# Cross-attention and a routed feed-forward layer: one division cut in two, one batch's projection in halves, and a wait for each half of the scores

## The chip, the cores and the metric

The kernel runs on one core of a Trainium2 chip. The metric is the device time of one execution in microseconds (us), of which the median of three runs is taken. A core has five engines with their own instruction streams: TensorE (PE; PEld is its weight load), VectorE (DVE), ScalarE (ACT), GpSimd (POOL) and SyncE (SP, which only issues transfers here). They wait for each other through semaphores.

## What is computed

Eight batches of 512 tokens of width 256 attend with 16 heads of width 16 to 1024 context tokens. Then the 128 best of the 512 tokens of each batch pass through a small transformer layer (causal attention among themselves, gated feed-forward of width 682) and replace their rows.

```python
x = x + xattn(layernorm(x), ctx, mask)          # 8 batches, 512 queries, 1024 keys, 16 heads of 16
#   q, k, v = x @ wq.T, ctx @ wk.T, ctx @ wv.T;  softmax(q k^T / 4) v;  @ wo.T
y = layernorm(x)
idx = top_k(y @ w_router, 128);  s = y[idx]
s = s + attention(rmsnorm(s, g1)) @ W_out.T     # causal, 128 tokens
s = s + (silu(h @ W1.T) * (h @ W2.T)) @ W3.T    # h = rmsnorm(s, g2)
out = x + y.at[idx].set(s)                       # y with the 128 chosen rows replaced
```

## The kernel before

**A batch is 32 steps.** A step `s` belongs to one group of four heads (`g = s // 8`) and one tile of 128 keys (`t = s % 8`). On PE it is, in this order: the scores of step `s` (`pe_scores`, L464: four heads, each in two column tiles, 32 rows by 64 columns of the array, into two of three pairs of PSUM banks); the values of step `s - 1` (`pe_values`, L486: four matmuls over all 128 rows, accumulated in `o_bank` over the eight key tiles); and then the "slot": work of the next batch's projections ("P"), of the same batch's late ones ("I", in batch 0 alone), or of the previous batch's feed-forward ("F"), which the table `PE_SLOT` (`PE_SLOT_0` for batch 0) puts at a step's number. ACT does the two exponentials of a step (`act_scores`, L506, one per pair of banks, 128x1024 each), and then what `ACT_SLOT` names. DVE follows `DVE_ORDER`, POOL `POOL_ORDER`. All orders are written out by hand, and every engine works strictly in its order.

**The ring of banks.** The three pairs are used in turn, two a step (`ring`, L443). The first pair of step `s` was last read by the second exponential of step `s - 2`, the second pair by the first exponential of step `s - 1`. Before L479 PE waits for both pairs; the values of step `s - 1` wait for the second exponential of step `s - 1` (L491).

**The slot's bank.** All work in slots goes through one bank, `m_bank` (`MISC`, 7). `take_bank` (L279) waits until the copy of the work before has freed it: ACT for keys ("K00" to "K11") and transposes ("xT", "hidT"), DVE for values ("V0" to "V3"), queries ("Q0", "Q1") and most of the feed-forward.

**The projection of the next batch** is ten products of 16 or 32 matmul records (4 K, 4 V, 2 Q) and two sets of transposes (xT). From batch 1 on, five of them are split over two steps (":0" and ":1"); in batch 0 each stands whole in one step, and of the steps 8 to 30 ten have a product, two have transposes, and 11 have nothing.

**The division.** `dve_norm` (L580) is done once for each group, after its last values: DVE transposes `o_bank` into `o_blk` and frees `o_bank`, takes the reciprocal of the sums, multiplies, and for an odd group transposes the result into `o_t`, which only the product with `wo` in the next batch reads. The division of group 1 ("norm1") falls into step 16. In the same step PE makes the feed-forward's keys ("k"), and in step 17 its values ("v"), its scores ("fs"), and the next batch's "V2". DVE's order is q, norm1, k, so that the copy of "k" out of `m_bank` (L773) comes after all four operations of norm1, and "v" needs that bank.

**The context** of a batch is loaded into one buffer, `ctx_in`, as soon as the last product that reads it has been copied out ("K10" and "V3" each add one to `ctx_free`), and read again by "K00:0" in step 31.

## Time and profile before

| what | value |
|---|---|
| median of three runs | 895.89 us (893.83 to 895.96) |
| the profiled execution | 896.05 us, its span 894.3 us |
| PE busy | 852.3 us, 95% of the span |
| ACT busy | 569.8 us, 64% |
| DVE busy | 313.4 us, 35% |
| POOL busy | 123.5 us, 14% |
| granted TensorE clock, mean | 0.993 of 2.4 GHz |

How to read it: PE is busy nearly everywhere up to the last batch's end, and the question for each microsecond is whether PE had an instruction that it could start. The step is the unit: the start of one step's scores to the next one's. The last 66 us, in which the last batch's feed-forward runs alone, are no part of the change.

### The profile page before, as it was taken

How to read it: one execution, taken by the hardware profiler on the slowest of the kernel's cores; microseconds unless marked ns; L12 is line 12 of the kernel's file. 1: busy time of each engine (PE TensorE's matmuls, PEld its weight loads, DVE VectorE, ACT ScalarE, POOL GpSimd, SP SyncE). 2: the span in 40 equal slices, each digit the busy share in tenths (PEclk: the TensorE clock that was granted, in tenths of full speed). 3: DMA queues.
4: the chain of work that ended last, by engine and by line, in shares of the span. 5: the costliest groups of instructions: out<-in, count | busy, mean ns of one | idle time of the engine just before them, and what ended most of it. 6: DMA issues, size and time to landing. Idle time of an engine off the chain costs nothing. (4 is left out here: it accounts for less than half of the span.)

```text
span 894.3 us, 28250 instructions
## 1 busy us (share of the span) xinstructions
PE 852.3 (95%) x11779; PEld 294.9 (33%) x11785; DVE 313.4 (35%) x918; ACT 569.8 (64%) x644; POOL 123.5 (14%) x175
## 2 busy tenths in 40 slices
PE   7999999999999999999999999999999999989774
PEld 2322232324323332334323333234323342224343
DVE  3132135421552226421553316422354214411631
ACT  3566767676677767666577766676576766776110
POOL 4000102020120102120120101101121100210110
PEclk9999999999999999999999999999999999999898
DMA  5060201210011200111011200102001100200000
GB/s 183 17 227 1 78 3 31 55 58 24 7 37 49 79 8 27 59 32 49 9 37 49 79 8 25 45 20 78 7 10 53 31 8 2 61 1 4 7 25 9
DMA packets 27577, 35.56 MB, mean 40 GB/s; under 512 B 2083, under 2 KB 24142, under 8 KB 27448
## 3 DMA queue, kind: packets, MB, share of 16 engines
q1 hardware_dynamic: 24952, 31.73, 11.2%
q0 software_dynamic: 2496, 1.98, 1.4%
q8 instruction: 96, 1.57, 0.7%
q14 instruction: 33, 0.27, 0.1%
HBM read 27.53 MB, written 8.93 MB: 41 GB/s over the span
## 5 line engine op out<-in xcount | busy, mean ns | idle before, releaser
L511 ACT ACTIVATE probs<-pair_bank 128x1024 f32<-128x1024 f32 x512 | 496.3, 1021 | 225.4 <-ACTq L510 225.4
L481 PE MATMUL pair_bank<-q_sb,k_sb 32*64 32x512 f32 x4096 | 286.4, 612 | 10.0 <-PEq L478 9.6
L500 PE MATMUL o_bank<-probs,va 128*32 128x512 f32 x2048 | 273.3, 604 | 1.3 <-ACT probs L511 1.1
L500 PEld LDWEIGHTS o_bank<-probs,va 128*32 128x32 f32 x2048 | 41.5, 108 | 205.4 <-issue 114.2
L481 PEld LDWEIGHTS pair_bank<-q_sb,k_sb 32*64 32x64 f32 x4096 | 60.9, 129 | 145.0 <-issue 145.0
L266 PE MATMUL m_bank<-wv_sb,ctx_in 128*32 128x256 f32 x1024 | 61.5, 380 | 0.0
L266 PE MATMUL m_bank<-ctx_in,wk_sb 128*32 128x512 f32 x480 | 60.3, 592 | 0.0
L628 DVE TENSOR_SCALAR va<-m_bank,valid 128x256 f32<-128x256 f32 x64 | 28.1, 480 | 91.6 <-DVEq L625 91.6
L586 DVE STREAM_TRANSPOSE o_blk<-o_bank 128x512 f32<-128x512 f32 x32 | 22.9, 717 | 92.7 <-DVEq L585 92.7
L266 PEld LDWEIGHTS m_bank<-hid_t,w 128*32 128x32 f32 x1392 | 39.5, 110 | 17.0 <-issue 16.0
L266 PEld LDWEIGHTS m_bank<-wv_sb,ctx_in 128*32 128x32 f32 x1024 | 33.5, 110 | 34.2 <-issue 18.9
L266 PE MATMUL m_bank<-hid_t,w 128*32 128x128 f32 x1392 | 43.3, 273 | 0.5 <-PEq L281 0.5
L896 POOL DMA_INDIRECT in_order<-y_tok,place x28 | 29.2, 1044 | 68.3 <-POOLq L895 58.2
L904 POOL DMA_INDIRECT out_dram<-att,row_of x8 | 13.2, 1647 | 171.3 <-POOLq L903 171.3
L888 POOL TENSOR_SCALAR_AFFINE_SELECT p_f<-p_f 128x1024 f32<-128x1024 f32 x16 | 17.5, 1094 | 123.8 <-POOLq L886 122.8
L266 PE MATMUL m_bank<-xn_t,wq_sb 128*32 128x512 f32 x240 | 30.7, 592 | 0.0
L872 POOL TENSOR_TENSOR mask_in<-mask_in,mask_row 128x256 int32<-128x256 int32 x32 | 23.4, 765 | 46.3 <-POOLq L869 46.3
L276 PE MATMUL o_bank<-before 128*128 128x512 bf16 x95 | 26.4, 435 | 3.3 <-POOL before L988 2.7
L798 DVE STREAM_TRANSPOSE o_blk<-m_bank 128x512 f32<-128x512 f32 x8 | 5.7, 717 | 65.1 <-DVEq L797 65.1
L266 PE MATMUL m_bank<-wo,o_t 128*32 128x256 f32 x448 | 27.1, 380 | 0.4 <-PEq L281 0.4
L266 PEld LDWEIGHTS m_bank<-ctx_in,wk_sb 128*32 128x32 f32 x480 | 15.3, 110 | 36.2 <-issue 36.2
L826 DVE SCALAR_TENSOR_TENSOR silu<-half_tanh,m_bank 128x384 f32<-128x384 f32 x15 | 8.3, 554 | 47.7 <-DVEq L825 47.7
(173 smaller groups left out, 604.1 us busy)
## 6 DMA issues: line engine op xcount, KB each, us to landing
ctx_in<-in_ctxT SPq DMA_DIRECT2D x7, 1024.0 KB, 5.0
x_in<-in_x SPq DMA_DIRECT2D x8, 512.0 KB, 4.0
x<-in_x SPq DMA_DIRECT2D x8, 512.0 KB, 4.3
mask_in<-in_mask SPq DMA_DIRECT2D x8, 512.0 KB, 3.9
out_dram<-base SPq DMA_DIRECT2D x8, 512.0 KB, 5.5
ctx_in<-in_ctxT SPq DMA_DIRECT2D x2, 512.0 KB, 7.5
mask_row<-in_mask SPq DMA_DIRECT2D x8, 128.0 KB, 3.9
x_tok<-in_order SPq DMA_DIRECT2D x7, 128.5 KB, 2.0
```

What stands on the lines that cost most here:

```text
L266: last = nc.tensor.matmul(dst[j], a[:, j], c, start=(begins and n == 0), stop=(ends and n == len(pairs) - 1))
L276: last = nc.tensor.matmul(dst, before[:, 0, 0:P], before[:, 1], start=True, stop=True)
L481: last = nc.tensor.matmul(pair_bank[pairs[r // 2]][j:j + 64, r % 2], key_tile(b, s, r)[:, j:j + 64], query_tile(b, s, r), start=True, stop ...
L500: last = nc.tensor.matmul(o_bank[32 * r:32 * r + 32], va[b % 2][:, t, HV * h:HV * h + 32], probs[s % 2][:, r], start=(t == 0), stop=(t == ...
L511: nc.scalar.activation(probs[s % 2][:, 2 * e:2 * e + 2, :], pair_bank[p][:], ACT.Exp, scale=HD ** -0.5).then_inc(s_free[p], 1)
L586: nc.vector.transpose(o_blk[:], o_bank[:]).then_inc(o_free, 1)
L628: last = nc.vector.tensor_scalar(by_head(va[b % 2][:, t])[:, :, 0:HD], bank[i][:, e * D:(e + 1) * D].rearrange("p (h d) -> p h d", h=H), o ...
L826: nc.vector.scalar_tensor_tensor(out=silu2[r][:], in0=half_tanh[r][:], scalar=1.0, in1=bank[i][:, 0:3 * P], op0=ALU.add, op1=ALU.mult).the ...
L872: last = nc.gpsimd.tensor_tensor(mask_words[:, t * WORDS:(t + 1) * WORDS], mask_words[:, t * WORDS:(t + 1) * WORDS], first, ALU.subtract)
L888: last = nc.gpsimd.affine_select(out=half, in_=half, compare_op=ALU.is_ge, fill=0.0, base=0, pattern=[[0, H8], [1, CAP]], channel_multipli ...
L896: nc.gpsimd.indirect_dma_start(in_order[:], bass.IndirectOffsetOnAxis(place[t][:, 0:1], 0), y_tok[:, t], None, bounds_check=CAP - 1, oob_i ...
L904: nc.gpsimd.indirect_dma_start(out.rearrange("b s d -> (b s) d"), bass.IndirectOffsetOnAxis(row_of[:, 0:1], 0), att[:], None, compute_op=A ...
```

## The change

It has three parts. First, "norm1" in `DVE_ORDER` becomes "norm1a" (the transpose out of `o_bank`), then "k", then "norm1b" (the other three operations). Second, `PE_SLOT_0` puts the projection of batch 1 in halves over the steps 8 to 29, one half a step, with a new `part` for V (the bank is taken by the first half, the signal given by the second); the transposes stand alone in steps 18 and 21; ACT's and DVE's tables follow. Third, in `pe_scores` the wait for the second pair of banks moves behind the first half's matmuls.

```diff
-             ("F", "base"), ("F", "q"), ("N", "norm1"), ("F", "k"), ("P", "V2"), ...
+             ("F", "base"), ("F", "q"), ("N", "norm1a"), ("F", "k"), ("N", "norm1b"), ("P", "V2"), ...

-             ..., ("I", "Q1", 6, False), ("P", "K00", 8, False), ("P", "K01", 9, False),
-             ("P", "K10", 10, False), ("P", "K11", 11, False), ("P", "V0", 12, False), ("P", "V1", 13, False),
-             ("P", "xT0", 15, False), ("P", "xT1", 17, False), ("P", "V2", 18, False), ("P", "Q0", 19, False),
-             ("P", "V3", 21, False), ("P", "Q1", 23, False), ("X", "K00:0", 31, False)]
-ACT_SLOT_0 = [("I", "K10", 2), ("I", "K11", 4), ("P", "K00", 8), ("P", "K01", 9), ("P", "K10", 10), ("P", "K11", 11),
-              ("P", "xT0", 15), ("P", "xT1", 17), ("P", "differ", 20)]
+             ..., ("I", "Q1", 6, False), ("P", "K00:0", 8, False),
+             ("P", "K00:1", 9, False), ("P", "K01:0", 10, False), ("P", "K01:1", 11, False), ("P", "K10:0", 12, False),
+             ("P", "K10:1", 13, False), ("P", "K11:0", 14, False), ("P", "K11:1", 15, False), ("P", "V0:0", 16, False),
+             ("P", "V0:1", 17, False), ("P", "xT0", 18, False), ("P", "V1:0", 19, False), ("P", "V1:1", 20, False),
+             ("P", "xT1", 21, False), ("P", "V2:0", 22, False), ("P", "V2:1", 23, False), ("P", "Q0:0", 24, False),
+             ("P", "Q0:1", 25, False), ("P", "V3:0", 26, False), ("P", "V3:1", 27, False), ("P", "Q1:0", 28, False),
+             ("P", "Q1:1", 29, False), ("X", "K00:0", 31, False)]
+ACT_SLOT_0 = [("I", "K10", 2), ("I", "K11", 4), ("P", "K00", 9), ("P", "K01", 11), ("P", "K10", 13), ("P", "K11", 15),
+              ("P", "xT0", 18), ("P", "differ", 20), ("P", "xT1", 21)]
-DVE_ORDER_0 = [..., ("P", "stats"), ("N", "norm0"), ("P", "xn"), ("P", "V0"),
-               ("P", "V1"), ("N", "norm1"), ("P", "V2"), ("P", "Q0"), ("P", "V3"), ("P", "Q1"), ("N", "norm2")]
+DVE_ORDER_0 = [..., ("P", "stats"), ("N", "norm0"), ("P", "xn"),
+               ("N", "norm1"), ("P", "V0"), ("P", "V1"), ("P", "V2"), ("N", "norm2"), ("P", "Q0"), ("P", "V3"), ("P", "Q1")]

             elif stage[0] == "V":
-                dst = take_bank(pe, i)
-                for e in range(2):
+                dst = bank[i] if part == 1 else take_bank(pe, i)
+                for e in share(part, 2):
...
-                last.then_inc(done["V"], 1)
+                if part != 0:
+                    last.then_inc(done["V"], 1)

             pairs = [ring(b, s, e) for e in range(2)]
-            for p in pairs:
-                pe.wait_ge(s_free[p], 1)
-                pe.sem_inc(s_free[p], -1)
             for r in range(HG):
+                if r % 2 == 0:
+                    pe.wait_ge(s_free[pairs[r // 2]], 1)
+                    pe.sem_inc(s_free[pairs[r // 2]], -1)
                 for j in range(0, P, 64):

-        def dve_norm(dve, b, g):
+        def dve_norm(dve, b, g, part=""):
-            dve.wait_ge(o_ready, 1)
-            dve.sem_inc(o_ready, -1)
-            nc.vector.transpose(o_blk[:], o_bank[:]).then_inc(o_free, 1)
-            dve.drain()
+            if part != "b":
+                dve.wait_ge(o_ready, 1)
+                dve.sem_inc(o_ready, -1)
+                nc.vector.transpose(o_blk[:], o_bank[:]).then_inc(o_free, 1)
+                dve.drain()
+            if part == "a":
+                return
```

## Rows read from the trace of the kernel before

**Rows 1.** Busy time by stretch: batch 0's steps 8-30, batch 1, batch 7.

```profile
46.92:116.29 69.37, 66.11 (x784) 17.47 (x785) 14.67 (x41) 48.99 (x55) 4.09 (x6) 1.00 0.25 86
119.19:222.38 103.19, 102.45 (x1460) 35.33 (x1456) 38.28 (x112) 70.71 (x81) 14.87 (x19) 1.00 0.12 37
735.36:828.00 92.64, 85.87 (x1224) 27.75 (x1224) 27.77 (x80) 66.37 (x73) 10.67 (x14) 1.00 0.07 18
```

**Rows 2.** PE's waits, whole span: us in total, times, longest us.

```profile
PE pair_bank L481 <- PEq L478: 9.6, 29, 1.3
PE m_bank L266 <- PEq L281: 3.6, 7, 0.7
```

**Rows 3.** Timeline, batch 0: scores of steps 20 (bare), 21 (whole V3), 22.

```profile
87.10 1.11 PE L481 MATMUL pair_bank<-q_sb,k_sb 32*64 32x512 f32 x16
...
89.51 1.12 PE L481 MATMUL pair_bank<-q_sb,k_sb 32*64 32x512 f32 x16 [0.30 <-PEq L478]
...
93.28 1.11 PE L481 MATMUL pair_bank<-q_sb,k_sb 32*64 32x512 f32 x16
```

**Rows 4.** Timeline, batch 1, PE alone: a step with half a product (Q1:0).

```profile
157.02 1.11 PE L481 MATMUL pair_bank<-q_sb,k_sb 32*64 32x512 f32 x16
158.07 1.07 PE L500 MATMUL o_bank<-probs,va 128*32 128x512 f32 x8
158.95 1.04 PE L266 MATMUL m_bank<-xn_t,wq_sb 128*32 128x512 f32 x8
159.92 1.11 PE L481 MATMUL pair_bank<-q_sb,k_sb 32*64 32x512 f32 x16
```

**Rows 5.** Timeline, batch 0: one bare step of a run of seven.

```profile
104.27 1.12 PE L481 MATMUL pair_bank<-q_sb,k_sb 32*64 32x512 f32 x16 [0.29 <-PEq L478]
105.32 1.06 PE L500 MATMUL o_bank<-probs,va 128*32 128x512 f32 x8
105.51 1.94 ACT L511 ACTIVATE probs<-pair_bank 128x1024 f32<-128x1024 f32 x2 [0.46 <-ACTq L510]
106.68 1.12 PE L481 MATMUL pair_bank<-q_sb,k_sb 32*64 32x512 f32 x16 [0.29 <-PEq L478]
```

**Rows 6.** Timeline, batch 7, step 17: scores that stood still in the middle.

```profile
780.86 1.07 PE L481 MATMUL pair_bank<-q_sb,k_sb 32*64 32x512 f32 x4
...
782.36 1.10 PE L481 MATMUL pair_bank<-q_sb,k_sb 32*64 32x512 f32 x12 [0.43 <-issue]
...
783.40 1.06 PE L500 MATMUL o_bank<-probs,va 128*32 128x512 f32 x8
```

**Rows 7.** Timeline, steps 16 and 17 of batch 1, then of batch 3.

```profile
170.44 0.72 DVE L586 STREAM_TRANSPOSE o_blk<-o_bank 128x512 f32<-128x512 f32 x1 [1.16 <-DVEq L585]
...
172.11 1.07 PE L500 MATMUL o_bank<-probs,va 128*32 128x512 f32 x8
...
173.34 0.42 DVE L773 COPY k_f<-m_bank 128x256 f32<-128x256 f32 x1 [0.55 <-DVEq L772]
...
173.92 1.07 PE L266 MATMUL m_bank<-wqkv,hid_t 128*32 128x256 f32 x16 [0.74 <-PEq L281]
...
377.71 1.07 PE L500 MATMUL o_bank<-probs,va 128*32 128x512 f32 x8
...
379.16 1.07 PE L266 MATMUL m_bank<-wqkv,hid_t 128*32 128x256 f32 x16 [0.39 <-PEq L281]
```

**Rows 8.** Timeline, batch 7: norm0, the chosen rows' norm, their transposes.

```profile
760.49 0.72 DVE L586 STREAM_TRANSPOSE o_blk<-o_bank 128x512 f32<-128x512 f32 x1 [1.27 <-DVEq L585]
...
773.57 0.48 DVE L757 SCALAR_TENSOR_TENSOR hid<-x_tok,ms,g_b 128x256 f32<-128x256 f32 x1 [1.24 <-DVEq L756]
...
774.66 0.44 PE L257 MATMUL m_bank<-ident,hid 128*128 128x128 f32 x2
```

**Rows 9.** Timeline, batch 0, step 20: ACT's check of the mask.

```profile
90.17 1.06 ACT L533 ACTIVATE mask_in<-mask_in 128x1024 f32<-128x1024 int32 x1
```

**Rows 10.** Page, transfers: the context's load, KB and us to landing.

```profile
ctx_in<-in_ctxT SPq DMA_DIRECT2D x7, 1024.0 KB, 5.0
```

More of the change, by code:

```diff
@@ L65 @@
              ("F", "order1"), ("N", "norm0"), ("F", "order2"), ("F", "order3"), ("P", "Q0"), ("P", "V1"), ("F", "selected"), ("P", "Q1"),
[1 row of a table removed]
[1 row of a table added]
              ("N", "norm2"), ("F", "u0"), ("F", "w0"), ("F", "u1"), ("F", "w1"), ("F", "down")]
 PE_SLOT_0 = [("I", "V0", 0, False), ("I", "V1", 1, False), ("I", "K10", 2, False),
[4 rows of a table removed]
-ACT_SLOT_0 = [("I", "K10", 2), ("I", "K11", 4), ("P", "K00", 8), ("P", "K01", 9), ("P", "K10", 10), ("P", "K11", 11),
-              ("P", "xT0", 15), ("P", "xT1", 17), ("P", "differ", 20)]
-DVE_ORDER_0 = [("I", "V0"), ("I", "V1"), ("I", "V2"), ("I", "V3"), ("I", "Q1"), ("P", "stats"), ("N", "norm0"), ("P", "xn"), ("P", "V0"),
-               ("P", "V1"), ("N", "norm1"), ("P", "V2"), ("P", "Q0"), ("P", "V3"), ("P", "Q1"), ("N", "norm2")]
[7 rows of a table added]
+ACT_SLOT_0 = [("I", "K10", 2), ("I", "K11", 4), ("P", "K00", 9), ("P", "K01", 11), ("P", "K10", 13), ("P", "K11", 15),
+              ("P", "xT0", 18), ("P", "differ", 20), ("P", "xT1", 21)]
+DVE_ORDER_0 = [("I", "V0"), ("I", "V1"), ("I", "V2"), ("I", "V3"), ("I", "Q1"), ("P", "stats"), ("N", "norm0"), ("P", "xn"),
+               ("N", "norm1"), ("P", "V0"), ("P", "V1"), ("P", "V2"), ("N", "norm2"), ("P", "Q0"), ("P", "V3"), ("P", "Q1")]
 POOL_ORDER = [("F", "var"), ("P", "var"), ("F", "scatter"), ("F", "rms0"), ("F", "causal"), ("F", "rms1"), ("P", "differ"), ("F", "add")]
@@ L1094, in _ @@
                         elif kind == "N":
-                            dve_norm(dve, b, int(stage[4]))
+                            dve_norm(dve, b, int(stage[4]), stage[5:])
                         elif kind in ("P", "I"):
```

4 rows, old and new, of tables (DVE_ORDER, PE_SLOT_0) are left out of this document.

## The prediction, made before the changed kernel was run

> **What bounds the kernel now.** I read the busy times by stretch first. Batch 1 is a wall of PE work: 102.45 us of 103.19 [rows 1]. The steps 8 to 30 of batch 0 leave 69.37 - 66.11 = 3.3 us, and batch 7, which has no next batch to project for, leaves 92.64 - 85.87 = 6.8 us [rows 1]. So there is something to win in batch 0, in batch 7, and in whatever small wait each batch between still has. PE's own waits name them: 9.6 us in 29 waits for a pair of banks (L478), and 3.6 us in seven waits for `m_bank`, most of them one in each batch's step 17 [rows 2]. Then the timeline, with the start of each step's scores as the ruler. In batch 0 a step with nothing in its slot takes 89.51 - 87.10 = 2.41 us, one with a whole product 93.28 - 89.51 = 3.77 us [rows 3], and in batch 1 one with half a product 159.92 - 157.02 = 2.90 us [rows 4]. Two halves take 5.80 us, a whole and a bare step 6.18 us: a bare step is not PE's pace.
>
> Why it is not: scores start at 104.27, ACT's first exponential at 105.51 (1.24 us later), and the next step's scores at 106.68, which is 1.17 us after that exponential started and so just when it had freed the pair of banks [rows 5]. 1.24 + 1.17 = 2.41 us is a loop between PE and ACT. PE's own part is 1.05 us from scores to values [rows 5] and 0.88 us from values to what follows [rows 4], 1.93 us.
>
> **Part 1, batch 0 in halves.** All ten products become two halves in two steps, no matmul is added. Before, the stretch of steps 8 to 30 takes 69.37 us [rows 1]. After, it holds 20 steps with a half at 2.90 us [rows 4] and three others. The transposes stand alone in a step before and after, so their price cancels; so does the one step that stays bare (30). What is left is ten times (one whole plus one bare against two halves): 10 x (6.18 - 5.80) = 3.8 us, and by the rounded starts 3.7 us. Against it stands one collision. ACT's check of the mask (1.06 us, with its accumulator read some 1.3 us) [rows 9] now stands in step 20 beside half a product, and the short step 21 (transposes only) follows. ACT then has 1.94 + 1.3 us of work and 0.2 us of start against a 2.90 us step, so it falls some 0.5 us behind, and the scores of step 22 need its first exponential; the transposes' step leaves 0.2 to 0.3 us of this uncovered. Part 1: -3.7 + 0.3 = **-3.4 us**, between -3.8 and -2.5.
>
> What could be late there, one by one. The bank: a second half's copy by ACT starts after the second exponential and takes less than the scores and values (1.93 us) in front of the next half; batches 1 to 6 run the same pattern at 2.90 us [rows 4]. DVE: norm1 and norm2 now stand before V0 and Q0, each in the step in which its group ends, one step before the copy is due. The context: V3 moves from step 21 to 27, so the load for batch 2 is issued in step 28. It takes 5.0 us [rows 10]; K00:0 of step 31 comes three steps and 1.93 us after step 28's start, over 10 us, against some 1.3 + 5.0 us. Cover of 3 to 4 us; without it each microsecond late would be a microsecond. SP has nothing behind that load that batch 0 needs.
>
> **Part 2, norm1 around the copy of "k".** In batch 1 DVE transposes `o_bank` at 170.44 (0.72 us), then works off the other three operations, and copies "k" only at 173.34; "v" starts at 173.92, after PE stood still for 0.74 us [rows 7]. With the copy second, it can start when "k" is finished and the transpose is over, near 171.3, and ends near 171.8. The values of step 16 start at 172.11 and "v" could follow 0.88 us [rows 4] later, at 172.99: the wait is gone with 1 us to spare, and "v" moves 0.93 us. In batch 3 the same distance is 379.16 - 377.71 = 1.45 us instead of 0.88: 0.57 us [rows 7]. Batches 1 and 4 are of the first kind, 3, 5 and 6 of the second (2 too, though its values ran slow for another reason; I take 0.3). Batch 7 has no such wait: PE stood still for 1.5 us in the middle of its scores, with nothing to wait for (780.86 to 782.36) [rows 6], and the copy was done by then. What is late next: after "v" and "fs" V2 needs ACT's copy of "v", which now stands right behind the second exponential of step 17; I find it 0.1 to 0.2 us early. norm1b delays nobody: `o_t` is read a batch later, `o_bank` was freed by norm1a. Behind it on DVE waits V2's copy, 3 us later. Sum 2 x 0.93 + 3 x 0.57 + 0.3 = **-3.9 us**, between -2.5 and -4.5.
>
> **Part 3, a wait for each half.** It only matters where scores wait, that is in bare steps. The first half's pair was read by the second exponential of two steps before and is always free. The second half still starts at the old time, and the values behind it too: rows 6 show what values do when the second half of the scores comes late (782.36): they start at 783.40, 1.04 us later, no sooner, though the first half had run long before. So an isolated bare step wins nothing. The gain comes one step on: the first half of step s+1 is done early, so its first exponential starts right behind the second one of step s. Over two bare steps: exponential start, +1.17 second half, +1.04 values, +0.88 first half of the next, +1.24 its exponential = 4.33 us instead of 4.82. **0.48 us for each pair of neighbouring bare steps.** Batch 0 has after part 1 only single ones (7 and 30): nothing. Batches 1 to 6 have none. Batch 7: steps 18 and 19 are a pair (0.5 us); 21 and 23 are single; step 0 is followed by the product with `wo`, which waits for norm3 anyway. Steps 3 to 5 and 7 to 13 would give 1.9 us in four pairs, but behind them, in step 14, the transposes of the chosen rows wait for DVE and POOL: that chain runs from norm0 (760.49) to hid (773.57 + 0.48) and the transposes start at 774.66, 0.61 us after hid's end [rows 8]. The chain is set by norm0, that is by the values of step 7, which come 0.5 us earlier; of the 0.61 us a signal needs only some 0.15 (the second pair's wait above: 1.17 us less the exponential's 1.03), so another 0.45 us can go. Gain there 0.9 us, not 1.9. Part 3: **-1.4 us**, between 0 and -2.9.
>
> What the moved wait costs where nothing is waited for: no instruction is added, two of four stand four matmuls later. No row shows a wait in that place. PE idled before the scores in 29 of the 256 steps [rows 2]; in the other 227 two waits in a row cost nothing, so I take 0; bounds below.
>
> Sum: -3.4 - 3.9 - 1.4 = -8.7 us. The profiled execution took 896.05 us (span 894.3), so 887.35; it lies 0.16 above the median 895.89, so **887.2 us**. PE's clock is at its 2.4 GHz level in all three stretches (1.00) [rows 1] and is less idle after the change; I expect none of it to change.
>
> **Rivals.** (a) *The wait in the middle shows* (the slow side). Every step has its second wait between the matmuls of two heads. If PE's queue does not run ahead enough to hide it, each step pays. The price per step of which it decides: 8.7 / 256 = 0.034 us. The rows bound it between 0 (the 227 steps) and 0.29 us, the idle time of a bare step's wait [rows 5]; at 0.05 us it is +12.8 us, giving 900 us. Against: PE has 0.88 us of values and a slot in hand before each scores. The Trainium skill, "Advanced Engine Details and Errata" (Miscellaneous Facts, Network/Comms) gives 50 to 100 ns for a sequencer's read of a semaphore; if that stood in the open in each step, the estimate from that page would be 900 to 913 us. No row of this trace shows such a price in the open; if the 227 steps paid it, they hid it. (b) *The half waits give nothing*: values keep their time and batch 7 hangs on its chain of chosen rows throughout; 887.2 + 1.4 = 888.6. (c) *Batch 0 does not do what it says*: a copy out of `m_bank` or the context comes late and takes back most of part 1, 887.2 + 2.5 to 3.4 = 890.2. (d) *Batch 7's standstill of 1.5 us* [rows 6] was an accident of issue and falls elsewhere: 885.7. For it: nothing was waited for. Against: PE's instruction count before it is unchanged.
>
> **Chances.** Forecast 0.52, (a) 0.07, (b) 0.12, (c) 0.12, (d) 0.12, and 0.05 for less than a third of the gain, within 0.3% (2.7 us, about what a measurement of this kernel can tell from no change). The far ends of the three parts together give 896.05 - 11.2 - 0.16 = 884.7, and (d) could come on top, so the range begins at 884.2; it ends at (c) with part 2 at its small end as to one us, 891.2. That leaves out (a), the remainder and some of the tails. Faster by over 0.3% (below 893.2) 0.87, same 0.06, slower 0.07.
>
> **What would show it.** Right: batch 0's steps 8 to 30 span 66.0 us; `m_bank` waits at "v" gone (L281 from 3.6 us to near 0), step 17 at 5.87 us in batches 1 to 6; in batch 7's runs scores start in turns of some 1.9 and 2.4 us; PE idle at L257 before the transposes of step 14 in batch 7. Wrong: half steps longer than 2.90 us anywhere (rival a), a wait at L291 or L281 in batch 0 (rival c), batch 7 as long as before but for 0.5 us (b).

## The result, and the profile of the changed kernel

The changed kernel takes **887.21 us**, median of 4 runs (884.06 to 889.00); the kernel before, run beside it, 895.92 us (893.83 to 898.64). The ratio is 0.990, its 95% interval 0.9878 to 0.9922. The forecast was 887.2 us. The profiled execution of the changed kernel took 886.53 us, with a span of 884.8 us against 894.3 before.

Busy times by stretch, the same three stretches as in [rows 1], in the same columns (batch 0 from the scores of step 8 to those of step 31, batch 1, batch 7):

```profile
45.98:112.79 66.81, 66.72 (x788) 17.52 (x784) 15.05 (x42) 48.87 (x55) 4.08 (x6) 1.00 0.27 92
116.05:218.06 102.01, 102.01 (x1461) 35.25 (x1457) 38.30 (x112) 70.39 (x80) 14.85 (x19) 1.00 0.12 37
727.44:819.30 91.86, 89.40 (x1228) 29.72 (x1224) 27.78 (x80) 66.93 (x74) 11.04 (x14) 1.00 0.07 18
```

Batch 0's stretch went from 69.37 to 66.81 us and batch 1 from 103.19 to 102.01, with PE busy in all of it. Batch 7 went from 92.64 to 91.86. "Busy" needs care from here on: a group of matmuls counts as busy from its first start to its last end, so a stop in the middle of a group counts as work. Two such stops are told of below.

PE's waits, as in [rows 2] (us in total, times, longest us). The lines moved by 3 or 4: L485 is the scores' matmul (L481 before), L269 the products' (L266), L284 their wait (L281), L504 the values' (L500).

```profile
PE o_bank L504 <- issue: 1.3, 1, 1.3
PE m_bank L269 <- PEq L284: 1.1, 2, 0.6
PE pair_bank L485 <- PEq L483: 0.3, 1, 0.3
```

The 29 waits for a pair of banks (9.6 us) have become one of 0.3 us, and the seven for `m_bank` (3.6 us) two of 1.1 us in all. At the top stands a new one: 1.3 us ahead of the values, released by nothing ("issue").

Batch 1, steps 16 and 17, timeline of all engines (start, duration, engine, line, operation; idle time before it and what ended it in brackets), against [rows 7]:

```profile
167.07 0.72 DVE L591 STREAM_TRANSPOSE o_blk<-o_bank 128x512 f32<-128x512 f32 x1 [1.16 <-DVEq L590]
...
168.04 0.43 DVE L780 COPY k_f<-m_bank 128x256 f32<-128x256 f32 x1 [0.25 <-DVEq L779]
...
168.74 1.07 PE L504 MATMUL o_bank<-probs,va 128*32 128x512 f32 x8
...
169.62 1.05 PE L269 MATMUL m_bank<-wqkv,hid_t 128*32 128x256 f32 x16
```

The copy of "k" starts 0.97 us after the transpose instead of 2.90 us, and "v" (L269) follows the values by 0.88 us with no wait. Before it was 1.81 us, 0.74 of them a wait.

Batch 7, steps 3 to 5, a bare pair (3 and 4) with the wait at each half, against the bare step in [rows 5]:

```profile
738.36 1.11 PE L485 MATMUL pair_bank<-q_sb,k_sb 32*64 32x512 f32 x16
...
739.60 3.98 ACT L515 ACTIVATE probs<-pair_bank 128x1024 f32<-128x1024 f32 x4 [1.83 <-ACTq L514]
...
740.40 1.46 PE L485 MATMUL pair_bank<-q_sb,k_sb 32*64 32x512 f32 x16
...
742.78 1.11 PE L485 MATMUL pair_bank<-q_sb,k_sb 32*64 32x512 f32 x16
```

ACT runs four exponentials without a gap (3.98 us): the first half of the next scores was there in time. The scores start 2.04 and 2.38 us apart instead of 2.41 twice. The stretched 1.46 us of the second scores is the wait between its halves.

And the two stops. In batch 0, step 12, the scores take 2.26 us instead of 1.11, and the weight load in their middle stood 0.97 us with no wait that the profile names ("issue"). In batch 7, step 14, the values stop half way for 1.26 us, again with no named wait, and the transposes of the chosen rows (L260) come after them although `hid` (L764) had been ready since 766.08:

```profile
57.93 2.26 PE L485 MATMUL pair_bank<-q_sb,k_sb 32*64 32x512 f32 x16
...
59.12 0.19 PEld L485 LDWEIGHTS pair_bank<-q_sb,k_sb 32*64 32x64 f32 x3 [0.97 <-issue]
...
764.51 1.05 PE L504 MATMUL o_bank<-probs,va 128*32 128x512 f32 x4
...
765.60 0.48 DVE L764 SCALAR_TENSOR_TENSOR hid<-x_tok,ms,g_b 128x256 f32<-128x256 f32 x1 [1.24 <-DVEq L763]
...
766.82 1.05 PE L504 MATMUL o_bank<-probs,va 128*32 128x512 f32 x4 [1.26 <-issue]
...
767.80 0.44 PE L260 MATMUL m_bank<-ident,hid 128*128 128x128 f32 x2
```

The stop that the kernel before had in step 17 of batch 7 [rows 6] is gone.

Where the 9.5 us of span went, stretch by stretch. Each number is a difference between starts of scores in the two timelines; the experiments are shown for what follows (us; "b0 8-31" runs from the start of step 8 to that of step 31, and so on):

```
                  ahead  b0 0-8  b0 8-31  b0 31   b1      b2      b3      b4      b5      b6    b7 0-15 b7 15-20 b7 20-31 tail
before            18.74  28.18   69.37    2.90  103.19  102.63  102.62  102.97  102.62  102.14  39.67   17.51    33.14    68.58
changed           18.14  27.84   66.81    3.25  102.01  102.22  102.01  102.01  102.01  101.15  40.73   15.63    33.19    67.77
batch 0 alone     19.00  28.18   67.16    2.90  102.98  102.62  102.62  102.96  102.61  102.14  39.66   17.24    33.13    67.42
norm1 alone       18.34  28.18   69.37    2.90  102.24  102.47  102.03  102.03  102.02  101.54  39.66   16.69    33.60    68.19
half waits alone  18.05  27.84   68.08    3.24  103.12  102.60  102.60  102.95  102.60  101.74  39.15   16.22    33.31    68.50
no half waits     17.92  28.18   67.71    2.90  102.03  102.50  102.02  102.03  102.02  101.54  39.67   17.24    33.61    68.17
```

- *Batch 0 in halves:* -2.56 us, that is -3.70 us of its own and +1.14 us for the stop in step 12, which took 4.04 us where its neighbours take 2.90.
- *norm1 in two parts:* step 17 fell from 6.79 to 5.84 us in batches 1 and 4, from 6.44 to 5.84 in 3, 5 and 6, and by 0.4 to 6.06 in 2 (a short stop, 0.45 us before and 0.20 now, stands in that step): -4.1 us.
- *Step 1 of batch 1:* 4.12 to 3.91 us, -0.2 us. It goes with batch 0's new tables, not with norm1: e1 and e4 have 3.91, e2 still 4.12 (though e7, with all three parts, has 4.06).
- *Half waits:* the last step of batch 6 -0.37, batch 7's steps 0 to 14 -0.52 (39.67 to 39.15, read from the kernel with the half waits alone, which has no stop there), steps 15 to 19 -0.44 (17.51 less the old stop of 1.44 is 16.07, now 15.63): -1.33 us.
- *Stops:* one of 1.44 us went, two of 1.14 and about 1.5 us came: +1.2 us.
- *Outside the change:* -0.60 us ahead of the first scores and -0.81 us behind the last. In the tail the kernel before was granted a lower clock in that execution, 0.57 of full speed over 8 us against 1.00 in the same place of the changed kernel (PEclk is the third number from the end), so most of that stretch ran at the 1.2 GHz level (the other tails of the table, from 67.42 to 68.50, vary as much):

```profile
840.00:848.00 8.00, 6.42 (x20) 3.00 (x21) 7.28 (x31) 0.00 (x0) 0.00 (x0) 0.57 0.00 0
```
```profile
831.00:839.00 8.00, 6.02 (x29) 2.83 (x29) 7.47 (x31) 0.00 (x0) 0.00 (x0) 1.00 0.00 0
```

The first is before, the second the changed kernel. Sum: -3.7 - 4.1 - 0.2 - 1.3 + 1.2 - 1.4 = -9.5 us.

### The profile page after: what moved, and what is told of

Its sections match the earlier page's. It is cut to its first block and busy times, and to the rows that moved or that the text cites. A ratio compares the mean times of both kernels' runs of the same rounds, so it can differ in the third digit from the quotient of the medians.

```text
span 884.8 us, 28257 instructions
## 1 busy us (share of the span) xinstructions
PE 853.4 (96%) x11779; PEld 296.7 (34%) x11785; DVE 313.2 (35%) x918; ACT 569.6 (64%) x644; POOL 123.3 (14%) x175
## 5 line engine op out<-in xcount | busy, mean ns | idle before, releaser
L485 PE MATMUL pair_bank<-q_sb,k_sb 32*64 32x512 f32 x4096 | 291.3, 612 | 0.4 <-PEq L483 0.3
L504 PE MATMUL o_bank<-probs,va 128*32 128x512 f32 x2048 | 274.2, 604 | 2.7 <-issue 1.3
L504 PEld LDWEIGHTS o_bank<-probs,va 128*32 128x32 f32 x2048 | 41.7, 108 | 207.5 <-issue 112.9
L485 PEld LDWEIGHTS pair_bank<-q_sb,k_sb 32*64 32x64 f32 x4096 | 62.8, 129 | 134.6 <-issue 133.4
L269 PE MATMUL m_bank<-wv_sb,ctx_in 128*32 128x256 f32 x1024 | 62.2, 380 | 0.0
L269 PE MATMUL m_bank<-ctx_in,wk_sb 128*32 128x512 f32 x480 | 61.0, 592 | 0.0
L269 PEld LDWEIGHTS m_bank<-wv_sb,ctx_in 128*32 128x32 f32 x1024 | 33.4, 110 | 36.0 <-issue 21.3
L269 PEld LDWEIGHTS m_bank<-hid_t,w 128*32 128x32 f32 x1392 | 39.4, 110 | 17.2 <-issue 16.3
L269 PE MATMUL m_bank<-hid_t,w 128*32 128x128 f32 x1392 | 43.4, 273 | 0.5 <-PEq L284 0.5
L269 PE MATMUL m_bank<-xn_t,wq_sb 128*32 128x512 f32 x240 | 31.1, 592 | 0.0
L269 PE MATMUL m_bank<-wo,o_t 128*32 128x256 f32 x448 | 26.9, 380 | 0.6 <-PEq L284 0.6
L269 PEld LDWEIGHTS m_bank<-ctx_in,wk_sb 128*32 128x32 f32 x480 | 15.3, 110 | 36.2 <-issue 36.2
```

What stands on the lines that cost most here:

```text
L269: last = nc.tensor.matmul(dst[j], a[:, j], c, start=(begins and n == 0), stop=(ends and n == len(pairs) - 1))
L485: last = nc.tensor.matmul(pair_bank[pairs[r // 2]][j:j + 64, r % 2], key_tile(b, s, r)[:, j:j + 64], query_tile(b, s, r), start=True, stop ...
L504: last = nc.tensor.matmul(o_bank[32 * r:32 * r + 32], va[b % 2][:, t, HV * h:HV * h + 32], probs[s % 2][:, r], start=(t == 0), stop=(t == ...
```

## The experiments

Three sets, each on one chip with its own runs of the kernel before: 895.45 us in the first set (23 runs), 905.95 in the second (21, one of them an outlier of 2880.69 us), 904.28 in the third (7). The second and third sets ran on chips on which both kernels take some 9 us longer, so only ratios cross from one set to another. All kernels compute the whole result.

### First set: the three parts

**e1, batch 0 alone.** The new tables of batch 0 and "V" in halves; `norm1` whole, both waits ahead:

```
-   ("N", "norm1a"), ("F", "k"), ("N", "norm1b"),
+   ("N", "norm1"), ("F", "k"),
...
+            for p in pairs:
+                pe.wait_ge(s_free[p], 1)
+                pe.sem_inc(s_free[p], -1)
```

> Only batch 0's projection in halves, the rest as before. Theory A (fill): a half in a bare step costs 0.49 us over the bare 2.41, so ten pairs of whole and bare (6.18 us) become 5.80; steps 8 to 30 of batch 0 take 66.0 us instead of 69.4, or about 1.2 us more if PE stands still once without a wait as it did in the changed kernel (step 12: 4.04 instead of 2.90). Everything from batch 1 on is unchanged. Time 3.4 us below before, 2.2 with a standstill. Rival B: the gain of batch 0 in the changed kernel came from the half waits (steps 7 and 30 show 2.04 us there): then the stretch here would be above 68 us and the time within 1 us of before.

Measured: 893.03 us, ratio 0.9981 (0.9969 to 0.9993). Its stretch of steps 8 to 30 takes 67.16 us: 2.21 less than before, with a stop of 1.43 us in the same step 12 (4.33 us); without it -3.64. The batches behind are those of before within 0.3 us; the tail is 1.16 us shorter, which the edit does not touch.

**e2, norm1 alone.** The order with `norm1a`, "k", `norm1b` and the function for it, nothing else:

```
-("F", "q"), ("N", "norm1"), ("F", "k"),
+("F", "q"), ("N", "norm1a"), ("F", "k"), ("N", "norm1b"),
```

> Only norm1 cut in two around the copy of k. Theory A: step 17 goes from 6.79 or 6.44 us to 5.84 in batches 1 to 6 (the wait for m_bank before v goes), 4.1 us in all; batch 7 only changes if its standstill of 1.5 us in step 17 falls elsewhere. Time 4 us below before, 5.5 if the standstill goes. Rival B: the wait for m_bank turns into one for the copy of v by ScalarE before V2, or for the free pair before the scores of step 18: step 17 would stay above 6.1 us and the time fall by 2 us or less.

Measured: 891.11 us, ratio 0.9952 (0.9937 to 0.9968). Batches 1 to 6 lose 3.84 us, step 17 takes 5.84 us there too, but 6.30 in batch 2, where the short stop is 0.43 us in this run. In batch 7 the steps 15 to 19 take 0.82 us less, because the stop in step 17 is 0.62 us there instead of 1.45, and 0.46 of it comes back in the next stretch. The same place, another length.

**e3, the half waits alone.**

```
-            for p in pairs:
-                pe.wait_ge(s_free[p], 1)
-                pe.sem_inc(s_free[p], -1)
             for r in range(HG):
+                if r % 2 == 0:
+                    pe.wait_ge(s_free[pairs[r // 2]], 1)
+                    pe.sem_inc(s_free[pairs[r // 2]], -1)
```

> Only the wait for each half of the scores. Theory A: a bare step next to another is worth 0.48 us a pair, a single one nothing. Batch 0 has here a run of seven bare steps (24 to 30), 14 and 16 with transposes between, 20 and 22 single: three pairs, 1.4 us, and 0.5 at most from 14 to 17. Batch 7 gains 0.5 us in steps 18 and 19 and up to 0.9 before the transposes of step 14. Time 2 to 3.3 us below before. Rival B (the wait in the middle shows): each filled step (2.90, 3.35, 3.77) is longer by 0.03 us or more, and the time is 8 us or more above that; filled steps of the changed kernel are equal to before within 0.01 us, which speaks against it. Rival C: nothing at all, the values wait instead; time as before.

Measured: 892.85 us, ratio 0.9969 (0.9958 to 0.9981). Here batch 0 still has its run of seven bare steps, 24 to 30. PE and ACT in four steps of it:

```profile
100.69 1.46 PE L481 MATMUL pair_bank<-q_sb,k_sb 32*64 32x512 f32 x16
102.08 1.06 PE L500 MATMUL o_bank<-probs,va 128*32 128x512 f32 x8
103.08 1.12 PE L481 MATMUL pair_bank<-q_sb,k_sb 32*64 32x512 f32 x16
104.13 1.06 PE L500 MATMUL o_bank<-probs,va 128*32 128x512 f32 x8
105.12 1.46 PE L481 MATMUL pair_bank<-q_sb,k_sb 32*64 32x512 f32 x16
```

103.08 + 2.04 = 105.12 is the short step, 100.69 to 103.08 the long one with 2.39 us: a pair takes **4.43 us**, not the 4.33 of the sum, against 4.82 before. It is 0.39 us for a pair, not 0.48. The rows say where the 0.10 us is: I had taken 0.88 us from values to what follows, from a row in which a product follows [rows 4]. Here scores follow, and it is 1.00 us (102.08 to 103.08; 0.99 in the next step). Values and products both use weights of 128x32, scores 32x64, so the dearer step is the one between the shapes (from product to scores it is 0.97 us in [rows 4]). The Trainium skill, "TensorEngine Tiling (Array Packing)", Key Properties, says that a change of the tiling mode drains the TensorE. The trace agrees in kind; its price, here about 0.11 us, was not measured by itself.

**e4, the changed kernel with both waits ahead again** (the edit of e3 backwards).

> The changed kernel with both waits ahead of the scores again. Theory A: batch 0 and batches 1 to 5 as in the changed kernel (one bare step alone gives nothing), batch 6 0.4 us longer (its last step), batch 7 as before apart from standstills: time 0.5 to 1.5 us above the changed kernel, some 888.5. Rival B: the half waits carry much of the gain; time 890 or more. Rival C: the half waits cost something in batch 7 (its step 14 waits 2.5 us longer in the changed kernel than before): time equal to or below the changed kernel's 887.2.

Measured: 888.94 us, ratio 0.9929 (0.9911 to 0.9946). So batch 0 and norm1 make 0.71%. The changed kernel's 0.990 (0.9878 to 0.9922) was measured in another session, and the two intervals overlap a little: that the half waits add 0.3% is shown by e3, not by this difference alone. It has both the stop of batch 0's step 12 (4.88 us) and the old one of batch 7's step 17. The single effects add up: -0.19, -0.48 and -0.31% make -0.98%, and the whole change has -1.0%.

### Second set: the price of the wait in the middle, batch 7's chain, the stops

**e5, the wait in the middle doubled.** A semaphore that PE raises, waits for and lowers itself, between the halves of every scores:

```
                 if r % 2 == 0:
                     pe.wait_ge(s_free[pairs[r // 2]], 1)
                     pe.sem_inc(s_free[pairs[r // 2]], -1)
+                if r == 2:
+                    pe.sem_inc(mid_sem, 1)
+                    pe.wait_ge(mid_sem, 1)
+                    pe.sem_inc(mid_sem, -1)
```

> The changed kernel with one more semaphore step between the two halves of every scores: TensorE raises a semaphore of its own, waits for it and lowers it again, 256 times. Theory A (hidden): TensorE's queue runs ahead, filled steps stay at 2.90, 3.35 and 3.77 us; only where the second half is waited for (the bare steps of batch 7) does it show, 0.1 us each at most. Time within 1.5 us of the changed kernel. Rival B (a wait in the middle is paid in the open): every step grows by what it costs, some 0.05 to 0.1 us, the time by 13 us or more, and then the one wait that the change moved there has cost something too.

Measured: 902.11 us, ratio 0.9958 (0.9945 to 0.9971), where the changed kernel in the same set has 0.9893; the span is 7.4 us longer. Neither theory had it. Nearly all steps with half or a whole product take 2.90 and 3.77 us as without it; the price is paid where the second half of the scores was waited for. The second step of a bare pair, in batch 7, starts of scores 740.91 and 743.60:

```profile
740.91 1.76 PE L490 MATMUL pair_bank<-q_sb,k_sb 32*64 32x512 f32 x16
742.61 1.06 PE L509 MATMUL o_bank<-probs,va 128*32 128x512 f32 x8
743.60 1.11 PE L490 MATMUL pair_bank<-q_sb,k_sb 32*64 32x512 f32 x16
```

It takes 2.69 us instead of 2.39, and the scores 1.76 instead of 1.46: three semaphore instructions, 0.30 us in the open. About the same 0.3 us shows in steps 15 and 25 of the batches between (2.91 to 3.19 and 3.35 to 3.63), which follow the bare steps 14 and 24, and 0.06 to 0.07 us in steps 7 and 9, nothing in the others. Rival (a) asked whether such instructions show in a filled step. The one that the change moves does not (2.90 and 3.77 us before and after); three more do in four of a batch's 32 steps.

**e6, the ranks first in batch 7.** The steps 0 to 14 of batch 7 hang on DVE's chain to `hid`; here `norm0` stands behind `order3` in batch 7, so that the chain does not wait for the values of step 7:

```
+DVE_ORDER_7 = [e for e in DVE_ORDER if e != ("N", "norm0")]
+DVE_ORDER_7.insert(DVE_ORDER_7.index(("F", "order3")) + 1, ("N", "norm0"))
```

> The changed kernel, but in batch 7 VectorE computes the ranks of the last two token tiles (order2, order3) before the division of group 0 instead of after it. Theory A (step 14 of batch 7 waits for the chain of the chosen rows, which norm0 holds up): norm0 and its wait for the values of step 7 (about 2.7 us) drop out of that chain, hid comes some 2.5 us earlier, TensorE does not wait in step 14 apart from a standstill, and batch 7's steps 0 to 14 take about 1.3 us less (the 0.4 us of each pair of bare steps from 7 to 13 now counts). Time 1 to 1.5 us below the changed kernel. Rival B: the transposes of step 14 were late only by the standstill; then nothing changes but a few tenths.

Measured: 894.71 us, ratio 0.9870 (0.9847 to 0.9893); the unchanged kernel beside it 0.9893 (0.9871 to 0.9914). The transposes no longer wait (step 14 takes 2.41 us), but the group's bank is freed late:

```profile
762.98 0.72 DVE L594 STREAM_TRANSPOSE o_blk<-o_bank 128x512 f32<-128x512 f32 x1 [0.20 <-issue]
...
763.80 1.24 PE L507 MATMUL o_bank<-probs,va 128*32 128x512 f32 x8 [1.32 <-issue]
```

The transpose that empties `o_bank` starts at 762.98; the scores of step 9 had begun at 761.36 and the values (L507) follow only at 763.80, 1.32 us late, and step 9 takes 3.61 us. The gain of one wait became another: steps 0 to 14 take 40.41 us against 40.83.

**e7, PE's stream shifted by 64 instructions.** 32 pairs of a raise and a lowering ahead of PE's first matmul, nothing else, so that every later instruction stands 64 places further on:

```
+                for _ in range(32):
+                    pe.sem_inc(pad_sem, 1)
+                    pe.sem_inc(pad_sem, -1)
```

> The changed kernel with 64 semaphore instructions of TensorE (up and down on one of its own) ahead of its first matmul, where it waits anyway for the first data. Theory A (TensorE's standstills without a wait belong to places of its instruction stream): the one of 1.1 us in step 12 of batch 0, which sits at the same weight load (number 578) in the changed kernel and in both kernels with batch 0 in halves, moves to a weight load some 30 earlier (64 instructions are 32 pairs of load and matmul), that is one step earlier, or vanishes; so does the one in step 14 of batch 7. Rival B (they belong to the moment or to what the other engines do): it stays in step 12. The time may go either way by 1 to 2 us.

Measured: 907.63 us, ratio 1.0001 (0.9977 to 1.0025). The pairs themselves make PE's first matmul start at 10.63 us instead of 2.66, and the first scores at 24.95 instead of 18.00 (e8): 6.95 us of the loss. Most of the rest is the stops, and they moved. Counted in PE's weight loads, the stop of batch 0 stands in front of load 578 in the changed kernel and in front of load 547 here: 31 loads, and with a matmul for each, 62 instructions. Its step is now 11 and takes 8.33 us. PE stood for 2.83 us behind its 14th matmul (3.84 from weight load to weight load), and afterwards the granted clock fell: 0.64 of full speed in the mean of the 4.5 us behind, so the 1.2 GHz level for most of them, in which a group of values takes 1.76 us instead of 1.07. That makes the other 1.6 us:

```profile
61.81 1.11 PE L486 MATMUL pair_bank<-q_sb,k_sb 32*64 32x512 f32 x14
65.74 1.07 PE L486 MATMUL pair_bank<-q_sb,k_sb 32*64 32x512 f32 x2 [2.83 <-issue]
66.74 1.76 PE L505 MATMUL o_bank<-probs,va 128*32 128x512 f32 x8
```
```profile
65.70:70.20 4.50, 4.46 (x26) 0.83 (x28) 0.00 (x0) 1.02 (x1) 0.00 (x0) 0.64 0.02 7
```

The stop of batch 7 moved too, from load 10406 to load 10375, again 31 loads: the values of step 14 run through, and the scores of step 13 take 2.39 us instead of 1.11:

```profile
783.15 2.39 PE L486 MATMUL pair_bank<-q_sb,k_sb 32*64 32x512 f32 x16
```

One new stop came, in step 17 of batch 3 (7.12 us instead of 5.84), and the short one in step 17 of batch 2 is gone (5.84 us instead of 6.34 in e8). So the stops belong to places in PE's instruction stream, not to what the matmuls do there.

**e8, the changed kernel again,** as the set's own mark.

> The changed kernel once more, for its time beside the three others on the same chip and to see whether its two standstills (step 12 of batch 0, step 14 of batch 7) come back at the same places. Theory A: they do, within 0.5 us of their length; the time is within 1.5 us of 887.2. Rival B: they fall elsewhere.

Measured: 896.22 us, ratio 0.9893 (0.9871 to 0.9914), about the same as on the first chip (0.990). The stop at load 578 is there (3.50 us), the one at load 10406 too (774.00 to 776.07). What is new on this chip is step 11 of batches 1 to 6: 5.35 us instead of 3.77. DVE's copy of Q0 out of the bank starts 1.95 us after the scores of step 11 (149.22), where on the first chip it is 0.25 (149.90 and 150.15); the wait in front of it is 3.89 us instead of 2.19, and PE waits for the bank:

```profile
151.17 0.75 DVE L646 TENSOR_SCALAR q_sb<-m_bank,parity 128x512 f32<-128x512 f32 x1 [3.89 <-DVEq L645]
...
152.72 0.64 PE L269 MATMUL m_bank<-wv_sb,ctx_in 128*32 128x256 f32 x8 [1.40 <-PEq L284]
```

Six such steps are 9.5 us, and the changed kernel's span is 9.7 us longer there (894.4 against 884.8). The kernel before is 10.5 us slower on that chip by its median; that it loses them in the same place is likely, but no profile of it was taken there. Why the copy starts late stays open; no run was made for it.

### Third set: is a stop's price to be had back?

**e9, norm0 in two parts in batch 7.** The division of the second group, applied to the first: only the half that frees the bank stands ahead of `order3`:

```
+DVE_ORDER_7 = [e for e in DVE_ORDER if e != ("N", "norm0")]
+DVE_ORDER_7.insert(DVE_ORDER_7.index(("F", "order2")) + 1, ("N", "norm0a"))
+DVE_ORDER_7.insert(DVE_ORDER_7.index(("F", "order3")) + 1, ("N", "norm0b"))
```

> The changed kernel, but in batch 7 the division of group 0 is cut too: order2 first (in the time in which VectorE waits for the values of step 7), then norm0a, order3, norm0b. Theory A (norm0 holds up the chain of the chosen rows; putting all of it behind order3, as in the kernel with the ranks first, frees o_bank too late for the values of step 8, and step 9 took 3.61 us instead of 2.40 for it): both waits go. Step 9 at 2.4 us or less, step 14 at 2.41 apart from standstills, batch 7's steps 0 to 14 at about 38 us (39.2 in the kernel with the half waits alone, 40.8 in the changed kernel). Time 1 to 2 us below the changed kernel beside it. Rival B: batch 7 is bound by TensorE and ScalarE alone; no difference.

Measured: 894.51 us, ratio 0.9890 (0.9874 to 0.9907), beside 0.9901 (0.9885 to 0.9918) for the changed kernel: the intervals overlap, so the time alone does not show a gain. Steps 0 to 14 take 38.79 us instead of 40.74, but most of that is the long stop, absent here; e3, whose step 14 has no long stop either, takes 39.15, so the edit's own part is some 0.4 us:

```profile
772.63 0.48 DVE L768 SCALAR_TENSOR_TENSOR hid<-x_tok,ms,g_b 128x256 f32<-128x256 f32 x1 [1.23 <-DVEq L767]
...
774.98 0.44 PE L264 MATMUL m_bank<-ident,hid 128*128 128x128 f32 x2
```

The transpose of `o_bank` for `norm0a` starts at 761.59, behind a wait of 0.28 us. `hid` is ready at 773.11 (772.63 + 0.48), the transposes come 1.87 us later, behind values that run in one piece: they no longer hang on the chain, and no step of batch 7 has a stop of a microsecond. I had expected 38 us; about 0.35 us of the difference is a short stop. That the long one at load 10406 is absent here, though the count of PE's instructions is the same, was not foreseen: a place is needed for a stop, but it is not enough. The old stop stands in front of load 10528, and each execution has at most one of the two. At 10528 the kernel before stood for 1.45 us, e1 and e4 for 1.17, e2 for 0.62, e11 for 0.34 and e3 for 0.31; at 10406 the changed kernel, e8, e10 and e12 stood for 2.1 to 2.3 (from load to load); e5, e6 and e9 did at neither. What sets their length is told under e10, with the packets of instructions.

**e10, the FFN's weights later.** The ten loads of the FFN's weights and gains (before, all issued by SP ahead of the batches) are issued in batch 0 behind the mask's load for batch 1:

```
+                def load_weights():
+                    sp.wait_ge(w_zero, 1)
+                    sp.sem_inc(w_zero, -1)
+                    sp.dma_start(wo[:], ...).then_inc(w_in["ffn_w"], 16)
...
+                    if b == 0:
+                        load_weights()
```

> The changed kernel with the ten loads of the feed-forward's weights (3.5 MB) issued after batch 1's mask, near 85 us, instead of at 43 us; they are needed at 116 us. Theory A (TensorE's standstill near 58 us in step 12 of batch 0, 0.3 to 2 us, comes from its instructions being fetched behind those loads): step 12 takes 2.90 us, batch 0's steps 8 to 30 take 65.7 us instead of 66 to 67, and the time falls by 0.3 to 1.5 us, unless the next block of instructions falls into the loads at their new place. Rival B: the standstill belongs to the place in the stream alone and stays.

Measured: 894.84 us, ratio 0.9890 (0.9874 to 0.9907), an interval that overlaps the changed kernel's. The stop in batch 0 is gone, step 12 takes 2.90 us (57.98 to 60.88), and steps 8 to 30 take **65.67 us**. PE of this kernel, and then what the DMA engines moved from 55 to 61 us, in the changed kernel and in this one (queue: packets, MB, share of 16 engines):

```profile
57.98 1.11 PE L485 MATMUL pair_bank<-q_sb,k_sb 32*64 32x512 f32 x16
...
60.88 1.11 PE L485 MATMUL pair_bank<-q_sb,k_sb 32*64 32x512 f32 x16
```
```profile
q1 hardware_dynamic: 820, 0.79, 42.1%
q8 instruction: 1, 0.02, 0.9%
```
```profile
q1 hardware_dynamic: 75, 0.07, 3.3%
q8 instruction: 1, 0.02, 1.0%
```

So the stop in batch 0 needs its place in the stream (e7) and goes when the loads beside it go (e10). But the two together are not enough: e5 has the same loads beside that place (51.6% of the DMA engines' time from 55 to 61 us) and no stop, and so has the kernel before (57.8%).

The traces hold the missing piece, the packets of queue q8, of kind "instruction" and 16 KB each. Here are the two of the long stops of batch 7: the packet that started between 764 and 765 us in the changed kernel, and the one between 780 and 781 us in the kernel before (6.0 and 5.5% of 16 engines in 1 us are 0.97 and 0.88 us of one packet):

```profile
q8 instruction: 1, 0.02, 6.0%
```
```profile
q8 instruction: 1, 0.02, 5.5%
```

The times in full (us; the place is PE's instruction number, with matmuls, weight loads and semaphore instructions counted as the trace records them):

```
kernel     place   PE reaches it  packet of q8     its end + 1.45   PE goes on
before    21952      780.91      780.10 - 780.98       782.43         782.36
changed    1216       58.02       56.74 -  57.62        59.07          59.12
changed   21696      764.54      764.38 - 765.35       766.80         766.82
e4         1216       57.78       57.01 -  58.22        59.67          59.72
e7         1216       61.90       63.42 -  64.31        65.76          65.74
e8        21696      774.00      773.64 - 774.51       775.96         776.07
e9        21696      774.01      771.33 - 772.54       773.99         no stop
before     1216       59.27       55.26 -  56.18        57.63         no stop
e5         1216       57.39       54.37 -  55.31        56.76         no stop
e10        1216       58.07       52.62 -  53.61        55.06         no stop
```

In all kernels together there are 34 stops of 0.28 us or more at the places of loads 578, 3400, 10283, 10406, 10528 and 10650 and e7's three, the short one of batch 2 among them. Each ends 1.23 to 1.64 us after a packet of q8 has ended, and their instruction numbers (1216, 7104, 10176, 21440, 21696, 21952 and 22208, all but one to within 2) are multiples of 256 apart. The reading that fits all of it: such a stop ends when a block of PE's instructions has arrived, and its length is set by how late the packet comes, which is also why the same place has a stop of 2.1 us in one kernel and none in another. The loads bear on that: with the weights moved away (e10, e11) the packet for place 1216 starts at 52.62 and 53.23 us, with them at 54.37 to 57.82 (63.42 in e7, which starts later). This is read from the order of events in fourteen traces; no run moved a packet by itself. What makes the packets late in batch 7, where no weights are loaded, stays open.

**e11, both.** The edits of e9 and e10 together.

> Both of the two before together. If their reasons are right the gains add: 1.5 to 3 us below the changed kernel beside it.

Measured: 894.10 us, ratio 0.9882 (0.9865 to 0.9898). It has 65.67 us in batch 0 and 38.80 us in batch 7's steps 0 to 14. Its median is 1.71 us under that of e12, but the intervals overlap, so the claim that it beats the changed kernel rests on the two stretches of its profile (1.14 and 1.94 us less), of which 0.50 us came back in steps 15 to 19 of batch 7 and 0.70 us ahead of the first scores.

**e12, the changed kernel a third time.**

> The changed kernel again, as the neighbour of the three others on this chip. If this chip is of the first kind, about 887 us with step 11 of batches 1 to 6 at 3.77 us; if of the second (step 11 at 5.35 us), about 896.

Measured: 895.81 us, ratio 0.9901 (0.9885 to 0.9918). Both stops are there (4.05 us in step 12, 40.74 us for steps 0 to 14).

## Why the prediction was right, and where it was not

**The total** of 887.2 us is the measured one to 0.01, which is better than the sum deserves. The three parts came to -9.1 us of the forecast -8.7; the stops gave 1.2 us back, and in the profiled execution 1.4 us fell off in places that the change does not touch. The two nearly cancel.

**Part 1, forecast -3.4, measured -3.70 us** (e10, where no stop disturbs it: 65.67 us, forecast 66.0). The sum "ten times a whole and a bare step against two halves" (3.7 to 3.8) was right to 0.1. The collision of ACT's check of the mask with half a product, priced at 0.3 us, cost 0.02: step 22 takes 2.92 us. My working let ACT fall 0.5 us behind; it fell 0.25 behind (its exponentials start 1.25 us after the scores in step 20, 1.50 in steps 21 and 22), and only 0.02 us of that reached PE. The context's load and DVE's copies were covered, as argued: every half step takes 2.90 us. Rival (c) is out.

**Part 2, forecast -3.9, measured -4.1 us.** The first kind came at 0.95 (forecast 0.93), the second at 0.60 (0.57), batch 2 at 0.4 (0.3); of that 0.4 the shorter stop made 0.25, and e2 has only 0.14 there. e2 shows the same 5.84 us alone in the other five. The 0.2 us of batch 1's step 1, which the forecast did not have, belongs to part 1's edit by e1 and e2. Nothing became late next: V2 starts without a wait.

**Part 3, forecast -1.4, measured -1.33 us.** The loop was right: an isolated bare step wins nothing (2.04 us and then 3.25, together the old 5.3), a pair wins. The term that was mis-sized is the pair, 0.48 forecast and 0.39 measured, by the 0.11 us between values and scores that I had read from a row in which a product followed. In batch 7 the chain of chosen rows held the gain of the first four pairs to 0.9 us, as forecast; 0.37 of it stand in the last step of batch 6, 0.52 in steps 0 to 14 of batch 7. Rival (b) is out by e4 as well: without the half waits the ratio is 0.9929.

**Rival (a)** is out: filled steps take the same 2.90 and 3.77 us, and e5 shows that most of them hide three more such instructions. The estimate of 900 to 913 us that stood beside it, from the Trainium skill, "Advanced Engine Details and Errata" (Miscellaneous Facts, Network/Comms), needs the read in the open. In the open such instructions do cost about that or a little more: 0.30 us for three in e5, 0.1 us each, and in e7 the first matmul starts 7.97 us later for 64, at least 0.12 us each. In most filled steps they cost nothing.

**Rival (d)** came true in its first half: the old stop of 1.44 us went. What spoke against it, "the count of instructions before it is unchanged", was no protection. But it gave no 1.5 us, since two other stops appeared. The trace of before could not show them, but its stop (and the slow values of batch 2, which I had put down to "another reason") came 1.4 us behind a packet of instructions, a hint that PE's stream has such places, and a term of "0, between -1.5 and +3" for them would have been the honest one.

## What to carry to other kernels

Read a busy engine's time step by step, not by its share: half steps filled alike gave back what full and empty ones lost. A wait moved between two halves of a group cost nothing in filled steps here; more semaphore instructions cost 0.1 us each where the engine was waiting anyway. When you take a duration "from the end of A to B" for a sum, take it from a row in which the same kind of B follows. And when an engine stands still with nothing to wait for, look whether the place stays the same from run to run, and whether a packet of instructions ended shortly before the engine went on, before you put it down to chance, or to the edit.

## What the runs showed of the hardware that I had not expected

- PE stood still for up to 3.84 us at fixed places of its instruction stream. The one at load 578 is the same in six executions of four kernels (changed three times, e1, e4, e9), 3.50 to 4.88 us for a step of 2.90; e6 has a short one there, 3.22. It stands 62 instructions earlier when 64 were put in front.
- 34 such stops end 1.23 to 1.64 us after a 16 KB packet of queue q8 ("instruction"), at instruction numbers that are multiples of 256 apart. With the weights loaded beside it the packet for place 1216 started at 54.37 to 57.82 us, without them at 52.62 and 53.23.
- From values to a product 0.88 us, from values to scores 0.99 to 1.00: some 0.11 us where the shape of the weights changes between 128x32 and 32x64.
- Semaphore instructions on PE: 0.1 us each in the open (0.30 us for three in e5; at least 0.12 each in e7), 0.00 in most steps with a product.
- After PE had stood for 3.84 us in e7 the granted clock was 0.64 in the mean of 4.5 us, and values took 1.76 us instead of 1.07.
- Two chips can differ by 1% in a single place of a kernel: step 11 of a batch takes 3.77 us on one, 5.35 on a second and 5.25 on a third.
